# Attention's two score passes two head groups apart instead of three

## What is computed

```python
x = _layernorm(hidden_states, ln1_g, ln1_b)
Q = jnp.einsum('bsd,dhr,hre->bhse', x, q_U, q_V) + q_b[None, :, None, :]
...
scores = jnp.einsum('bhse,bhte->bhst', Q, K) * scale
causal = jnp.tril(jnp.ones((S, S), bool))
scores = jnp.where(causal[None, None], scores, jnp.asarray(-1000000000.0, scores.dtype))
attn = jax.nn.softmax(scores, axis=-1)
ctx = jnp.einsum('bhst,bhtd->bhsd', attn, V)
```

## Time and profile before

| | us |
|---|---|
| median of three executions | 750.95 (746.2 to 752.59) |
| the profiled execution, its own time | 749.43 |
| its span, first to last instruction | 747.6 |
| PE busy | 624.8 (84%) |
| DVE busy | 443.2 (59%) |
| ACT busy | 421.0 (56%) |
| POOL busy | 304.7 (41%) |
| first unit of the second pass of group 0 | at 75.40 |
| first unit of the second pass of group 31 | at 384.93 |

### The profile page before, as it was taken

The page is one execution under the profiler, slowest core; times in us unless marked ns, Lnnn a source line. Parts: engine busy times, 40 slices in busy tenths (PEclk is TensorE's granted clock), DMA queues, the critical chain, the costliest instruction groups (busy, mean ns, idle before and its releaser), DMA issues.

```text
span 747.6 us, 15319 instructions
## 1 busy us (share of the span) xinstructions
PE 624.8 (84%) x5334; PEld 413.5 (55%) x5365; DVE 443.2 (59%) x1306; ACT 421.0 (56%) x749; POOL 304.7 (41%) x490
## 2 busy tenths in 40 slices
PE   4756899998998989999979777887976999999940
PEld 3523444444444544444436464666746899999930
DVE  2689687878788766777606676666741222222227
ACT  5321667676666657666675767775423555555510
POOL 4141424143433415131314276755740454455541
PEclk9958999999999999999999988998997999999975
DMA  8542232333243423331834112111163777777827
GB/s 176 190 162 75 80 123 98 133 133 108 100 158 108 150 91 132 133 106 50 247 118 126 54 46 73 52 47 44 59 164 95 228 229 230 229 226 228 229 104 267
DMA packets 85853, 100.97 MB, mean 135 GB/s; under 512 B 12960, under 2 KB 68040, under 8 KB 85680
## 3 DMA queue, kind: packets, MB, share of 16 engines
q1 hardware_dynamic: 76752, 87.19, 37.9%
q0 software_dynamic: 4544, 9.45, 3.5%
q10 hardware_dynamic: 4480, 3.35, 1.9%
HBM read 60.28 MB, written 37.57 MB: 131 GB/s over the span
## 4 chain that ended last, share of the span: by engine, by line
PE 52%; DVE 12%; DMA 10%; SPq 8%; issue 6%; POOL 5%; ACT 5%; another core or an unknown queue 0%; POOLq 0%; ACTq 0%; DVEq 0%
PE ps_r L1438 8%; PE ps_s L1428 8%; PE ps_pv L1253 7%; DVE row_max L1620 4%; PE ps_r L1208 4%; PE ps_pv L1324 3%; PE ps_r L1205 3%; PE ps_s L1316 3%; DMA arena<-slots_d 3%; PE ps_s L1236 2%; PE ps_r L1346 2%; PE ps_s L1332 2%; DMA k_d<-arena_early 2%; PE ps_pv L1346 2%; PE ps_r L1183 2%
## 5 line engine op out<-in xcount | busy, mean ns | idle before, releaser
L1620 DVE TENSOR_REDUCE row_max<-ps_r 128x1 f32<-128x384 f32 (+3 forms) x384 | 207.0, 595 | 67.6 <-PE ps_r L1208 59.5
L958 ACT ACTIVATE arena<-ps_s 128x1024 f32<-128x1024 f32 (+1 forms) x192 | 159.1, 880 | 64.0 <-PE ps_s L1236 63.1
L1205 PE MATMUL ps_r<-later_q,ident_b 128*128 128x128 bf16 (+1 forms) x384 | 92.5, 247 | 29.8 <-DVE row_max L1620 18.2
L926 POOL DMA_INDIRECT y_d<-arena,target x78 | 74.7, 957 | 94.8 <-DVE arena L1813 82.6
L1208 PE MATMUL ps_r<-arena 128*128 128x128 bf16 (+3 forms) x481 | 112.1, 302 | 0.0
L1205 PEld LDWEIGHTS ps_r<-later_q,ident_b 128*128 128x128 bf16 x384 | 36.1, 98 | 90.2 <-DVE row_max L1620 43.5
L1253 PE MATMUL ps_pv<-arena 128*32 128x512 f32 (+3 forms) x1024 | 83.3, 444 | 0.1
L1809 DVE TENSOR_TENSOR arena<-ps_r,arena_early 128x256 f32<-128x256 f32 x39 | 16.6, 425 | 107.6 <-PE ps_r L1438 107.6
L880 POOL DMA_INDIRECT slots_d<-arena,slots x64 | 65.0, 1015 | 27.5 <-issue 17.7
L1236 PE MATMUL ps_s<-arena 51*128 51x256 bf16 (+3 forms) x512 | 60.2, 300 | 0.0
L1208 PEld LDWEIGHTS ps_r<-arena 128*128 128x128 bf16 x512 | 51.3, 100 | 13.9 <-issue 3.2
(11 more groups left out here) (221 smaller groups left out, 1113.1 us busy)
## 6 DMA issues: line engine op xcount, KB each, us to landing
arena<-in_ew SPq DMA_DIRECT2D x30, 514.0 KB
ctx_d<-ctx_raw SPq DMA_DIRECT2D x32, 256.0 KB, 3.4
arena<-q_d SPq DMA_DIRECT2D x64, 102.0 KB
arena<-k_d SPq DMA_DIRECT2D x64, 96.0 KB
arena<-slots_d SPq DMA_DIRECT2D x39, 132.0 KB, 3.2
arena_early<-in_ew SPq DMA_DIRECT2D x9, 514.0 KB
arena<-y_d SPq DMA_DIRECT2D x8, 512.0 KB, 6.2
q_d<-arena_early SPq DMA_DIRECT2D x8, 384.0 KB, 3.0
```

Of the source, the lines that this page charges most:

```text
L926: pool.indirect_dma_start(y_d[:], bass.IndirectOffsetOnAxis(ap=target[:, k, c:c + 1], axis=0), res[:, k, c, :], None).then_inc(put[k], 16)
L958: act.activation(dst, src, ACT.Exp, scale=SCALE).then_inc(exp_done, 1)
L1205: pe.matmul(diag, ident_b[:], later_q[:].unsqueeze(1).to_broadcast([P, len(js), P]), start=True, stop=False, skip_group_check=True)
L1620: dve.reduce_max(row_max[:, m % 2, js[0] % 2, j:j + len(js), i], src, AXIS.X).then_inc(max_taken, 1)
```

## The change

```diff
 NG = B * GROUPS
-LAG = 3
+LAG = 2
 FIRST_STEP, LAST_STEP = -9, NG + 7
```

## The result

With two groups of distance the kernel takes 813.94 us (median of 4, 811.84 to 815.82) against 751.68 (median of 4, 746.2 to 752.59): 1.083 times the time before, 95% interval 1.080 to 1.087. The profiled execution took 815.82 us, with a span of 814.0 against 747.6. Medians here are of all executions of a run; ratios and intervals leave out its slow ones, those over 1.5% above the fastest.

A forecast was written before the change was run, and what follows sets the result against it. PE's woven list was taken to bound the attention, with DVE's row maxima close behind. Terms 44.8 + 5.3 + 15.1 + 0 + 8 = 73 on the profiled 749.4 gave 823, by the median 824 us; range 790 to 856.

The forecast's parts named there:

- The mechanism: Attention: the maxima's chain of copy, store and load must close within one step, so PE's second pass waits for it.
- Steps 4 to 23: Middle of the attention: five four-step patterns of 50.05 us, 250.3 us instead of 205.5, +44.8.
- 0 mod 4: Attention steps like 12: 1.7 load to pass, 6.82 to ACT's copy, 5.58 trip (store issued to both loads issued), 14.1 us.
- 1 mod 4: Attention steps like 13: 1.7 load to pass, 5.46 to ACT's copy, 3.29 from store to both loads issued, 10.45 us.
- 2 mod 4: Attention steps like 14: SP's 13 stack and context loads, 9.64 us, plus 4.46 from store to both loads issued, 14.1.
- 3 mod 4: Attention steps like 15: 1.7 load to pass, 5.47 to ACT's copy, 4.23 from store to both loads issued, 11.4 us.
- the rival of shrinking trips: Attention: store-to-load times shrink to 3.29 us in every step as the same bytes have more time; 798 us, chance 0.22.
- The clock: PE in attention: clock falls to 0.50 after long idling, about 1.7 us lost nearly once a pattern; +8, between 0 and 30.
- The rival in which the clock falls in every stalled step: Attention: two more clock losses of 1.7 us per pattern, 17, and 5 in steps 0 to 3; 846 us, chance 0.15.
- The start: Up to group 0's second pass: SP's four stack loads hide the shorter run-up, 75.4 us as before; 0, between -5 and +3.
- Steps 0 to 3: First attention steps, no context to load yet: PE's side binds, 11.6 us each, 46.4 instead of 41.1, +5.3.
- Steps 24 to 30: End of the attention, with MLP loads ahead of step 28's store: 78.1 us instead of 63.0, +15.1.

The follow-up runs named there:

- the cut run: Two groups of distance, second pass neither waiting for the maxima nor subtracting them: 749.22 us, 0.999 times the kernel before.
- the fillers: Two groups, PE multiplying a constant 8 to 20 times ahead of the longest-waiting second passes: 805.34 us (1.053 times the kernel before), repeated 803.30 us (1.070).
- the first run: First of the two runs of the fillers on the two-group kernel: 805.34 us beside 759.9 for the kernel before, 1.053 times.

## Why the prediction was right

The forecast was 824 us; 814 came. A loss of 73 us was forecast, and by the medians it is 62. Point by point:

- *The mechanism.* Shown. The second pass waits for the DMA of its maxima in 22 steps, and without that wait the loss is nil (the cut run).
- *Steps 4 to 23.* 250.3 forecast without the clock, about 258 with it, 251.3 measured. By kind of step, five of each:

| steps | forecast, one | measured, one | measured, mean | error over five |
|---|---|---|---|---|
| 0 mod 4 | 14.1 | 11.3 to 12.8 | 11.9 | -10.8 |
| 1 mod 4 | 10.45 | 10.5 to 13.7 | 11.4 | +4.8 |
| 2 mod 4 | 14.1 | 13.7 to 16.0 | 14.6 | +2.6 |
| 3 mod 4 | 11.4 | 11.0 to 13.2 | 12.3 | +4.4 |

  That 250.3 and 251.3 lie so close is luck: one large error against three smaller ones. The large one is the trip of steps 0 mod 4, taken at step 12's 5.58 us. In the kernel before, the same kind of step already had 3.42 to 5.58 (one of the five in the earlier trace rows), and after the change it had 3.4 to 4.5, with ACT's copy at 6.1 to 6.4 instead of 6.82. SP's list in steps 2 mod 4 was as said, 13.7 and 13.8 us in steps 14 and 6, but 15.7 and 16.0 in 10 and 18, where the store came 3.6 and 4.5 us behind the copy instead of 2.4 to 2.5. Steps 1 mod 4 came at 10.5 in steps 5, 13 and 21, as said, and at 13.7 and 11.8 in 9 and 17, which begin at the low clock. In steps 3 mod 4 the trip was not the 4.23 taken over from before but 1.9 to 2.4 us, and the store landed after 1.4 to 1.9 us instead of 3.7 to 4.9. It now leaves 3.3 to 4.3 us behind the issue of SP's last stack load instead of 0.1, which I take for the reason. The low clock put PE's own work in the trip's place, and the step took 11.0 to 13.2. So the rival of shrinking trips came true by its condition: the mean trip of steps 4 to 23 fell from 4.5 to 3.5 us, near its 3.3. Its 798 us didn't come, because by the table the low clock and SP's lateness took the time instead.
- *The clock.* +8 forecast; the fillers' gain of 7.6 to 18.8 us in the attention holds that amount, no closer. It is on the chain in steps 9 and 17, where it put ACT's copy 2.7 and 1.4 us later, and in steps 3 mod 4 it stands in place of the trip and not on top of it.
- *The 11 us too many.* By the traces the loss is 66.4 us, 6.6 under the forecast of 73: some 7 of it are the steps 4 to 23 with the clock added, 2 the steps 24 to 30, 1 the steps 0 to 3, and against them stand 0.8 at the start and 2.2 behind the attention. The other 4 us are the choice of executions: the traced one lies 1.9 over the median after and 2.3 under it before.
- *Which steps the clock fell in.* The rival in which the clock falls in every stalled step came about in part: in steps 3 mod 4, in 9 and 17, and at the ends in 0, 29 and 31, not in the others.
- *Behind which waits.* Of the 24 waits for the maxima, the clock fell behind each of the 11 that were 2.1 us and longer, and behind none of the 13 of 1.4 and less (the waits here are those of the weight load). Other runs show no such clean border: in the change once more it fell also in step 10, 1.2 us after a wait of 0.9, with the maxima on ScalarE's queue behind 1.3, and with fillers it stayed up behind 2.3 and in the first run behind 2.6. The 3.5 us behind the wait of 3.61 and behind that of 0.42, columns as in rows 2 with the granted clock third from the end:

```profile
260.10:263.60 3.50, 3.44 (x25) 1.07 (x26) 0.02 (x1) 2.61 (x3) 0.00 (x0) 0.56 0.30 92
...
246.50:250.00 3.50, 3.50 (x44) 1.60 (x44) 2.61 (x7) 1.99 (x3) 1.44 (x6) 1.00 0.31 97
```

  Both are busy throughout, with 25 and 44 matmuls. The Trainium skill (TensorE: Matmul & The Clock Gate, "HAM oscillation — how this bites in real kernels") says that DMA waits in each tile make each tile start cold; the trace agrees for those 11 waits and not for the 13 short ones.
- *The start.* 0 forecast, +0.8 measured, and for the reason given: without the wait for the maxima group 0 starts at 71.24, and with SP's stack loads evened out at 70.54. The store went out at 70.50 instead of the forecast 68.6, and a trip of 4.4 instead of 5.1 made up for part of it.
- *Steps 0 to 3*: +5.3 forecast, +4.4 measured. *Steps 24 to 30*: +15.1 forecast, +13.1 measured, again by errors both ways: step 24 took 10.0 us instead of 12.9, step 28 16.8 instead of 17.4, step 29, at the low clock, 11.7 instead of 9.4, and step 30 8.7 instead of 10.2.
- *The part behind* was forecast not to change; it took 2.2 us more in the profiled execution.

## What to carry to other kernels

When two passes are joined by a small transfer, add up the transfer's whole round from the trace (work ahead of the store, the issuing queue's list, store landed, what the list has between store and load, load landed) and hold it against the step; what the profile shows as no wait at all may be one step away from being the bound. A distance larger than the round needs cost little here (the fourth group a run-up of 6.5 us, 6 to 10 at the end), one too small costs in most steps. And before the distance is blamed or changed, look at the issuing queue's list around the transfer: evening it out gave back 26 us of 62 at two groups (814 to 788), and with the MLP loads spread too 3 us at three. And don't size such a trip from one step: the same store and load took 1.9 to 6.0 us in the change's trace, by what stood between them and what else was under way.

## What I hadn't expected of the hardware

- The store of the maxima (48 x 128 bf16, 12 KB) and its load, alone on a second issuing queue, took as long as among SP's transfers: 3.7 us against 3.5 from store to load in the mean of steps 4 to 23, and in step 15 5.1 us from the store's issue to the load's and 3.5 more to land. The queue was not what made them slow.
- The landing of the same store had a median of 3.6 us before and 1.4 after, at nearly the same extremes (1.3 to 5.3, 1.3 to 5.4), with the same transfers in the program, only in another order in time.
- The granted clock fell to 0.50, the 1.2 GHz level, behind each wait for the maxima of 2.1 us and longer in the change's trace, and once soon after a wait of 0.9 us when the change ran again. Matmuls of constants put into the wait kept it up in most steps, for 10.7 us less in all by the medians, although PE does more work for it.
- The part behind the attention differed by 14 us between sets of runs (363 us from group 31 on in the run with three groups and the wait cut, 377 in the first one with fillers, which changes only the first step of it), so that the attention's gains of 3 to 6 us had to be read from the timeline.
